# Edge matrix of a graph layer: one-hots of two strips at a time, blocks innermost, on one Trainium2 core

## The reference, cut to what matters

```python
def _sage(x, src, dst, W_l, b_l, W_r):
    msg_sum = jax.ops.segment_sum(x[src], dst, num_segments=N_NODES)
    cnt = jax.ops.segment_sum(jnp.ones((src.shape[0],), x.dtype), dst, num_segments=N_NODES)
    aggr = msg_sum / jnp.maximum(cnt, 1.0)[:, None]
    return aggr @ W_l.T + b_l + x @ W_r.T
h_fwd = _sage(x, src, dst, W_l_f, b_l_f, W_r_f)
h_bwd = _sage(x, dst, src, W_l_b, b_l_b, W_r_b)
```

## Time and profile before

| | us |
|---|---|
| median of three runs | 1466.12 |
| profiled execution, span | 1467.1 |
| TensorE busy | 1177.5 |
| VectorE busy | 747.6 |
| GpSimd busy | 600.5 |
| ScalarE busy | 454.9 |

### The profile page before, as it was taken

How to read it: one execution, slowest core, us unless ns; L and a number is a source line. 1 busy time by engine, 2 the same in 40 slices (tenths; PEclk the granted TensorE clock), 3 DMA queues, 4 the chain that set the end, 5 groups by cost and what they waited for, 6 DMA issues and landing times. The chain is left out here.

```text
span 1467.1 us, 22800 instructions
## 1 busy us (share of the span) xinstructions
PE 1177.5 (80%) x7604; PEld 921.6 (63%) x7604; DVE 747.6 (51%) x2374; ACT 454.9 (31%) x916; POOL 600.5 (41%) x700
## 2 busy tenths in 40 slices
PE   3777789898428887076999999998998789975997
PEld 2677789366316665065777777776876465545886
DVE  5999961478763343643544444443445361233332
ACT  2577750432312222021333333333332234231110
POOL 3466630203415665006656666666566200002442
PEclk9899999999758999587999999999999989996999
DMA  5000000400432222654555555555555137366551
GB/s 121 1 2 2 2 2 2 112 4 1 129 138 75 84 78 60 146 172 144 170 153 169 163 168 164 171 171 170 159 175 173 38 101 229 89 162 205 171 186 53
DMA packets 97275, 165.62 MB, mean 113 GB/s; under 512 B 15505, under 2 KB 59181, under 8 KB 96773
## 3 DMA queue, kind: packets, MB, share of 16 engines
q1 hardware_dynamic: 71669, 90.69, 21.5%
q0 software_dynamic: 25488, 73.39, 16.5%
HBM read 138.40 MB, written 27.63 MB: 113 GB/s over the span
## 5 line engine op out<-in xcount | busy, mean ns | idle before, releaser
L2326 POOL DMA_INDIRECT em_gathered<-edge_table,el_which x313 | 302.7, 967 | 188.5 <-DVE em_hidden L2416 111.5
L2338 PE MATMUL em_projected<-em_w,em_attr 128*128 128x256 f32 x1252 | 295.9, 391 | 27.1 <-DVE em_hidden L2416 16.8
L2338 PEld LDWEIGHTS em_projected<-em_w,em_attr 128*128 128x128 f32 x1252 | 242.9, 196 | 72.3 <-issue 38.5
L2416 DVE TENSOR_TENSOR em_hidden<-em_projected,em_gathered 128x512 f32<-128x512 f32 (+1 forms) x157 | 107.4, 686 | 202.9 <-PE em_projected L2338 99.6
L2438 ACT ACTIVATE em_hidden<-em_hidden 128x512 f32<-128x512 f32 (+1 forms) x157 | 98.7, 629 | 262.1 <-DVE em_hidden L2416 221.6
L434 POOL TENSOR_SCALAR nm_hot_a<-nm_order,ek_places 128x125 bf16<-128x125 int16 x150 | 99.5, 671 | 52.1 <-PE nm_banks L558 49.2
L446 DVE TENSOR_SCALAR nm_hot_key<-nm_key_order,ek_keys 128x100 bf16<-128x100 int16 x500 | 118.8, 265 | 0.0
L2752 POOL DMA_INDIRECT oe_hidden<-oe_table,oo_node x27 | 26.0, 962 | 182.3 <-DMA oe_table<-state 130.9
L2838 PE MATMUL oe_banks<-oe_wd,xn_T 128*128 x432 | 99.3, 384 | 0.0
L445 DVE TENSOR_SCALAR nm_hot_a<-nm_order,ek_places 128x125 bf16<-128x125 int16 x350 | 94.9, 273 | 0.0
L2838 PEld LDWEIGHTS oe_banks<-oe_wd,xn_T 128*128 128x128 f32 x432 | 81.4, 193 | 10.3
(11 more groups left out here) (503 smaller groups left out, 2253.9 us busy)
## 6 DMA issues: line engine op xcount, KB each, us to landing
em_attr<-in_edge_attr_sets SPq DMA_DIRECT2D x156, 256.0 KB
oe_table<-state SPq DMA_DIRECT2D x20, 448.0 KB
oe_wd<-in_ffn_Wd SPq DMA_DIRECT2D x8, 1024.0 KB
em_gathered<-edge_table,el_which POOLq DMA_INDIRECT x313
mx_w<-in_ffn_w SPq DMA_DIRECT2D x16, 256.0 KB
oe_table<-state SPq DMA_DIRECT2D x1, 2248.8 KB
state<-in_x SPq DMA_DIRECT2D x5, 448.0 KB
state<-in_x SPq DMA_DIRECT2D x1, 2240.0 KB
```

Of the source, the lines that this page charges most:

```text
L2326: nc.gpsimd.indirect_dma_start(out=gathered[:, n % GATHERED, :], out_offset=None, in_=table, in_offset=bass.IndirectOffsetOnAxis(ap=lanes. ...
L2338: last = nc.tensor.matmul(projected[:, k % BANKS, n % 2, :], attr[:, k % ATTR_RING, (n % 2 * KB + f) * 128:(n % 2 * KB + f + 1) * 128], w1 ...
L2416: nc.vector.tensor_tensor(pair_slots(k), projected[:, k % BANKS, 0:width, :], gathered[:, at:at + width, :], ALU.add).then_inc(pre_ready, 1)
```

## The change

The one-hots of two strips (ten windows) are made by two comparisons of whole tensors on VectorE. The ten windows lie innermost, so in one partition `hot_a` is 125 x 10 and `hot_key` 100 x 10; the counting rows are stored ten times over (`order` 125 x 10, `key_order` 100 x 10, 16-bit integers), and the places and keys become 16-bit. A matmul reads one window's one-hots with a step of ten elements of two bytes. The ring holds three pairs of strips instead of four strips. GpSimd makes no one-hots. Of a tile's four batches of turned blocks ScalarE copies the first and the third, and VectorE the second and the fourth, behind the build of the pair that holds the strip of place 3 or 4 in the next tile; the counter of kept copies is split in two. `std` moves into an unused part of `adj`.

```diff
-        self.keys, self.places = sb("keys", [128, WINDOWS]), sb("places", [128, WINDOWS])
+        self.keys, self.places = sb("keys", [128, WINDOWS], BF16), sb("places", [128, WINDOWS], BF16)
...
-    BATCHES, RING = 4, 4
+    BATCHES, RING, JOINED = 4, 3, 2
+    HOTS = JOINED * PER_STRIP
...
-        order = sb("order", [128, P], I16)
-        key_order = sb("key_order", [128, TILES, WINDOW], I16)
+        order = sb("order", [128, P, HOTS], I16)
+        key_order = sb("key_order", [128, KEYS, HOTS], I16)
...
-        hot_a = sb("hot_a", [128, RING, PER_STRIP, P], BF16)
-        hot_key = sb("hot_key", [128, RING, PER_STRIP, KEYS], BF16)
+        hot_a = sb("hot_a", [128, RING, P, HOTS], BF16)
+        hot_key = sb("hot_key", [128, RING, KEYS, HOTS], BF16)
...
-                nc.gpsimd.iota(order[:], [[1, P]], base=0, channel_multiplier=0)
-                nc.gpsimd.iota(key_order[:], [[1, TILES], [TILES, WINDOW]], base=0, channel_multiplier=0).then_inc(made, 1)
+                nc.gpsimd.iota(order[:], [[1, P], [0, HOTS]], base=0, channel_multiplier=0)
+                nc.gpsimd.iota(key_order[:].rearrange("p (b d) n -> p b d n", d=WINDOW), [[1, TILES], [TILES, WINDOW], [0, HOTS]], base=0,
+                               channel_multiplier=0).then_inc(made, 1)
...
-                pool.wait_ge(keys_ready, 1)
-                for w_ in range(STRIPS):
-                    if w_ >= RING:
-                        pool.wait_ge(hot_used, w_ - RING + 1)
-                    for s in BY_POOL[w_ % 2]:
-                        n = w_ * PER_STRIP + s
-                        nc.gpsimd.tensor_scalar(hot_a[:, w_ % RING, s, :], order[:], ek.places[:, n:n + 1], None,
-                                                ALU.is_equal).then_inc(pool_hot_ready, 1)
...
-                def build(w_):
...
+                def build(i):
+                    if i >= RING:
+                        dve.wait_ge(hot_used, (i - RING + 1) * JOINED)
+                    at = slice(i * HOTS, (i + 1) * HOTS)
+                    for hot, numbers, found in ((hot_a, order, ek.places), (hot_key, key_order, ek.keys)):
+                        last = nc.vector.tensor_tensor(hot[:, i % RING], numbers[:],
+                                                       found[:, at].unsqueeze(1).broadcast_to([128, numbers.shape[1], HOTS]), ALU.is_equal)
                     last.then_inc(hot_ready, 1)
+
+                def keep_turned(t, j):
+                    n = t * BATCHES + j
+                    dve.wait_ge(turn_ready, n + 1)
+                    nc.vector.tensor_copy(adj[:P, t, j * BATCH * P:(j + 1) * BATCH * P].rearrange("p (b a) -> p b a", b=BATCH),
+                                          turned[:, n % 2, 0:BATCH * 128].rearrange("p (b a) -> p b a", b=BATCH)[:, :, 0:P]
+                                          ).then_inc(turn_kept[n % 2], 1)
...
-                for w_ in range(RING, STRIPS):
-                    build(w_)
-                    if w_ == PER_TILE:
+                for i in range(RING, STRIPS // JOINED):
+                    build(i)
+                    if i == RING:
                         ek.vector_last(dve)
-                    if w_ % PER_TILE == 2 and w_ >= 2 * PER_TILE:
-                        keep_total(w_ // PER_TILE - 2)
+                    for w_ in range(i * JOINED, (i + 1) * JOINED):
+                        t, j = w_ // PER_TILE - 1, w_ % PER_TILE - 2
+                        if t >= 0 and j in (1, 2):
+                            keep_turned(t, 2 * j - 1)
+                        if t >= 1 and j == 0:
+                            keep_total(t - 1)
                 keep_total(TILES - 2)
+                for j in (1, 3):
+                    keep_turned(TILES - 1, j)
                 keep_total(TILES - 1)
...
-                    pe.wait_ge(hot_ready, w_ + 1)
-                    pe.wait_ge(pool_hot_ready, pool_hots(w_ + 1))
+                    i, first = w_ // JOINED, w_ % JOINED * PER_STRIP
+                    pe.wait_ge(hot_ready, i + 1)
                     for s in range(PER_STRIP):
-                        last = nc.tensor.matmul(acc[:, w_ % 2, s * KEYS:(s + 1) * KEYS], hot_a[:, w_ % RING, s, :], hot_key[:, w_ % RING, s, :],
-                                                start=True, stop=True)
+                        last = nc.tensor.matmul(acc[:, w_ % 2, s * KEYS:(s + 1) * KEYS], hot_a[:, i % RING, :, first + s],
+                                                hot_key[:, i % RING, :, first + s], start=True, stop=True)
                     last.then_inc(hot_used, 1)
...
-                        pe.wait_ge(turn_kept, i - 1)
+                        pe.wait_ge(turn_kept[i % 2], i // 2)
...
-                    if t >= 0 and j < BATCHES:
+                    if t >= 0 and j in (0, 2):
                         keep_turned(t, j)
-                for j in range(BATCHES):
+                for j in (0, 2):
                     keep_turned(TILES - 1, j)
```

More of the change, by code:

```diff
@@ L368, in neighbour_sums @@
     nc = p.nc
-    BATCHES, RING = 4, 4
+    BATCHES, RING, JOINED = 4, 3, 2
+    HOTS = JOINED * PER_STRIP
     NORMS = ((0, 2), (2, CHUNKS))
-    BY_POOL = ((1,), (1, 3))
-    pool_hots = lambda w_: w_ // 2 * 3 + w_ % 2
     BATCH = TILES // BATCHES
@@ L380, in neighbour_sums @@
         w = sb("w", [128, KB, 2 * HALF])
-        order = sb("order", [128, P], I16)
-        key_order = sb("key_order", [128, TILES, WINDOW], I16)
+        order = sb("order", [128, P, HOTS], I16)
+        key_order = sb("key_order", [128, KEYS, HOTS], I16)
         ident = sb("ident", [P, P], F16)
-        hot_a = sb("hot_a", [128, RING, PER_STRIP, P], BF16)
-        hot_key = sb("hot_key", [128, RING, PER_STRIP, KEYS], BF16)
+        hot_a = sb("hot_a", [128, RING, P, HOTS], BF16)
+        hot_key = sb("hot_key", [128, RING, KEYS, HOTS], BF16)
         adj_T = sb("adj_T", [P, 2, TILES, P], F16)
-        mean, var, half, std = (sb(n, [P, TILES]) for n in ("mean", "var", "half", "std"))
+        mean, var, half = (sb(n, [P, TILES]) for n in ("mean", "var", "half"))
+        std = adj[:P, 1, 0:2 * TILES].bitcast(F32)
         banks = p.ps("nm_banks", [128, 8, 512], scope=scope)
@@ L399, in neighbour_sums @@
         made, hot_ready, hot_used = sem("made"), sem("hot_ready"), sem("hot_used")
-        pool_hot_ready, keys_ready = sem("pool_hot_ready"), sem("keys_ready")
-        window_kept, turn_ready, turn_kept = sem("window_kept"), sem("turn_ready"), sem("turn_kept")
+        keys_ready = sem("keys_ready")
+        window_kept, turn_ready, turn_kept = sem("window_kept"), sem("turn_ready"), [sem("even_turn_kept"), sem("odd_turn_kept")]
         total_ready, total_kept = sem("total_ready"), sem("total_kept")
@@ L427, in _ @@
                 nc.gpsimd.memset(parts[:, :, :, HALF:HALF + 1], 1.0).then_inc(made, 1)
-                pool.wait_ge(keys_ready, 1)
-                for w_ in range(STRIPS):
-                    if w_ >= RING:
-                        pool.wait_ge(hot_used, w_ - RING + 1)
-                    for s in BY_POOL[w_ % 2]:
-                        n = w_ * PER_STRIP + s
-                        nc.gpsimd.tensor_scalar(hot_a[:, w_ % RING, s, :], order[:], ek.places[:, n:n + 1], None,
-                                                ALU.is_equal).then_inc(pool_hot_ready, 1)
             @block.vector
             def _(dve):
-                def build(w_):
[L440 to L447, removed]
-                    last.then_inc(hot_ready, 1)
+                def build(i):
[5 more added lines that the diff above has]
+                                                       found[:, at].unsqueeze(1).broadcast_to([128, numbers.shape[1], HOTS]), ALU.is_equal)
+                    last.then_inc(hot_ready, 1)
+                def keep_turned(t, j):
[4 more added lines that the diff above has]
+                                          ).then_inc(turn_kept[n % 2], 1)
                 def keep_low(t):
@@ L633, in _ @@
                         turn(TILES - 1, j)
-                pe.wait_ge(turn_kept, TILES * BATCHES)
+                for kept in turn_kept:
+                    pe.wait_ge(kept, TILES * BATCHES // 2)
                 for b in range(TILES):
@@ L662, in keep_turned @@
                                          turned[:, i % 2, 0:BATCH * 128].rearrange("p (b a) -> p b a", b=BATCH)[:, :, 0:P],
-                                         ACT.Copy).then_inc(turn_kept, 1)
+                                         ACT.Copy).then_inc(turn_kept[i % 2], 1)
                 def root(n, first, last):
```

## The result

The changed kernel takes 1510.93 us (median of 4 runs, 1509.59 to 1512.33) against 1466.05 for the kernel before in the same session (4 runs): 1.0311 times, 95% interval 1.0292 to 1.0330. It is slower by 45 us where 15 us of gain were forecast, and outside the range. The profiled execution took 1512.33 us, with a span of 1510.6.

What follows compares the result with a forecast made beforehand. VectorE was taken to bound the 152 us edge-matrix stage; afterwards TensorE's 120.3 us, waits of 15.2 and 1.5 for start and tail gave 137, saving 15 us: 1451 us forecast, range 1432 to 1500.

Steps and rivals of the forecast that it cites:

- Matmul operands 20 bytes apart: TensorE's 500 counting matmuls: spread reads raise each from 58.6 to 100 ns, adding 21 us.
- the one row of spread reads: VectorE reduction over elements a tile apart: 640 in 1282 ns, 1.76 ns each, 1.7 times the adjacent price.
- the slower one: Counting matmuls (L558): each spread element costs its own time, 176 to 220 ns; stage 170 to 190, time 1484 to 1504; chance 0.27.
- It decides from where a counting matmul costs about 140 ns: Threshold for losing in the edge-matrix stage: 70 + 70 + 12 = 152 us, the stage's time before.
- The pair of comparisons: VectorE's one-hot builds: a pair for two strips takes 1.33 us, at 0.52 ns an element.
- The copy of 625: VectorE's copy of turned blocks out of PSUM: 0.73 us of spacing taken, 0.42 if the 16-bit form is half.
- VectorE as bound of the stage before: Edge-matrix stage: VectorE, never idle, sets the pace; a faster one could free 52 us.
- The new wait: VectorE queued behind TensorE's turns: TensorE idles 1.43 us in every second tile, 0.17 in others; about 15 us in all.
- The iotas: Two iotas at the start grow tenfold, 8.4 us at most; at worst the first gathers slip by 0.4 us.
- The stage starts at: Start of the edge-matrix stage: stays at 57.7 us, with three pairs prebuilt where four strips were.
- GpSimd is empty in it: Edge-matrix stage: GpSimd, which built 3 of 20 one-hots, has nothing left to do.

Runs made afterwards that it cites:

- e6: A separate program, not the network: groups of 64 counting-shape matmuls with operands 4 to 64 bytes apart; weights spread cost 60 ns at 4 bytes, 229 at 16.
- e1: Changed kernel with the counting matmul's moving operand read adjacent (wrong counts): stage 195.1 us, time 1509.0 us.
- e2: Changed kernel with the counting matmul's stationary operand read adjacent (wrong counts): stage 171.1 us, time 1488.52 us.
- e13: Changed kernel with all copies of turned blocks on ScalarE: stage 191.7 us, time 1508.18 us, 1.0252 of the kernel before.
- e14: Changed kernel with VectorE's copies of turned blocks one strip later, after the next build: stage 191.5 us, time 1508.44 us, 1.0243 of the kernel before.
- e5: Changed kernel with five blocks innermost instead of ten, a matmul step of 10 bytes: stage 163.3 us, time 1472.07 us against 1462.08 before.
- e3: Changed kernel with both counting-matmul operands read adjacent (wrong counts): stage 117.3 us, time 1434.93 us, 0.9743 of the kernel before.
- e4: Changed kernel with two blocks innermost instead of ten, a matmul step of 4 bytes: stage 118.2 us, time 1435.99 us, 0.9757 of the kernel before.
- e8: e4 with VectorE's copies of turned blocks one strip later, after the next build: stage 106.8 us, time 1414.92 us, 0.9686 of the kernel before.
- e9: Kernel before with only the shared copies of turned blocks added: stage 166.4 us, time 1392.93 us, 1.0125 of the kernel before.

## Why the prediction was wrong

**The failed step** is in "Matmul operands 20 bytes apart": "I take the ratio, 100 ns, as the engine normally moves its elements faster than VectorE, and expect it to keep part of that." TensorE keeps nothing of it. A counting matmul costs 219 ns in a row and 236 in a strip. The term was 21 us; at 236 it is 500 x (0.236 - 0.0586) = 89. I scaled the one row of spread reads the earlier trace rows as a ratio, when it was a time for each element. e6's 216 ns at 20 bytes is 125 x 1.73, nearly the row's 1.76 as it stood.

**The rival that came true** is the slower one, with its place (L558) and its upper price, 220 ns. Which operand sets it is answered by e1 and e2: the 125 weights. Its stage, 190, is close to what e13 and e14 have (191.7, 191.5), in part by luck: it was 180 of TensorE's work and 10 of idle time and ends, and they have 188 of work and hardly any idle time. The changed kernel has 204 because of its nine waits and of the fallen clock; no case had the latter. To its time, 1504, the stage's further 14 us are added, and the 8 that came back after the stage (51.9 - 43.5), most of them at L1484, go off: 1510. "It decides from where a counting matmul costs about 140 ns" holds in its direction: e5, with 144 ns for its step, has a stage 11 us above the kernel before, and a time 10 above. The sum behind it would give 70 + 72 + 12 = 154 for e5, and 163 was measured, with dearer comparisons and a clock of 0.94.

**The other steps.** The pair of comparisons: 1.33 forecast, 1.31 measured. The Trainium skill's estimate of 1.3 us by two elements a cycle (VectorE: DVE Perf Modes, perf-mode tier table) agrees. The copy of 625: 0.73 forecast, 0.40 measured, the lower end. The mistake was to let every PSUM row, all 32-bit, speak for a 16-bit one. VectorE as bound of the stage before: right, and the comparisons do free it (e3, e4: 34 us). The new wait: the mechanism is right, at 1.2 us in every second tile when reads are cheap, and 0.3 idle (0.48 lost) in the changed kernel, where TensorE has more work in hand. e8 removes it and confirms what was queued behind what. The iotas: the larger takes 1.59 us, where at most 4.2 was written, and the first gather starts at 9.68, earlier than before (9.99). The stage starts at 58.1 against 57.7 forecast. GpSimd is empty in it, as written.

**The sum, rebuilt from measured terms.** 1200 ordinary matmuls x 0.0586 = 70.3; 500 counting x 0.236 = 118; together 188.3. In e14 the fall of the clock before 73.4 adds about 2: 190, measured 191.5. In the changed kernel the nine waits add 4.3 and the falls of the clock about 10: 203, measured 203.8. These last two terms are read off its own strips, so they describe this run and foretell nothing.

## What to carry to other kernels

Price a TensorE operand by the 16-byte pieces it touches, some 1.84 ns each for the worse of the two operands, and compare that with what the matmul takes anyway: here up to some 32 pieces were free. When a layout must please an elementwise engine and TensorE, make the inner run just long enough for the first (two 16-bit elements here) rather than the whole batch. And put work that an engine takes over from another behind what the bound engine waits for next, not ahead of it; by itself, as in e9, it may cost more than it brings.

## What the runs showed of the hardware

- A spread operand costs TensorE by pieces of 16 bytes: no price at 4 bytes, 117 ns at 8, 229 at 16, and nothing more from there to 64 bytes. In a row of like matmuls the weight load and the moving read overlap, and the longer counts: at 16 bytes 229 ns with the weights spread, 179 with the moving operand, 230 with both. Where such a row meets other matmuls, the moving read costs some 0.1 us once (1.18 us for five, 1.07 in e1).
- Reads 20 bytes apart do not follow the clock, as the two strips above show; adjacent ones do. In e6 the adjacent group from 43.72 costs 58 ns a matmul at a granted clock of 1.00 and the one from 227.96 costs 89 ns (5.71 us for 64) at 0.62. Of the changed kernel's stage the clock slows only the other 1200 matmuls. The granted clock fell in e6 without any idle of TensorE.
- A comparison of int16 with a row-repeated int16 into bf16 with runs of two or ten elements takes 0.58 ns an element (1.31 us for 2250); with runs of five more (930 and 776 ns instead of 802 and 674), and with runs of one, 1.1 ns.
- A VectorE instruction that meets a run of GpSimd additions can last until the run ends: 6.64 us instead of 0.68, in some kernels and not in others. What decides which is open.
